# Two graph attention layers on one core: each gather waits for the landing of the third gather ahead of it

## The reference

```python
def layer0(x, src, dst):                 # edges sorted by dst
    h = layer_norm(x); q, k, v = h @ Wq + bq, h @ Wk + bk, h @ Wv + bv
    e = sum(q[dst] * k[src], -1) / 4     # per head, logits of each edge
    p = exp(e - segment_max(e, dst)[dst])
    a = p / segment_sum(p, dst)[dst]
    x = x + segment_sum(a * v[src], dst) @ Wo + bo
    return x + gelu(layer_norm(x) @ W1 + bf1) @ W2 + bf2

def layer1(x, src, dst, edge_attr):
    e = edge_attr @ We                   # added to k[src] and to v[src]
    ...                                  # the same attention, skip, norms and a feed-forward part
x = layer_norm(x + layer0(x, src, dst))
x = layer_norm(x + layer1(x, src, dst, edge_attr_64))
```

## Time and profile before

| what | before |
|---|---|
| median of three runs | 1345.44 us (1345.04 to 1345.83) |
| span of the profiled execution, from the first to the last instruction | 1659.7 us |
| VectorE busy in that span | 1039.2 us, 63% |
| TensorE busy | 914.0 us, 55% |
| GpSimd busy, 832 gathers among it | 898.0 us, 54% |
| ScalarE busy | 749.2 us, 45% |
| steady rounds of layer 0, batches 4 to 25 | 154 to 697 us |
| steady rounds of layer 1, batches 4 to 25 | 945 to 1523 us |

### The profile page before, as it was taken

One profiled execution on the slowest core, in us unless ns is written; L12 is line 12 of the kernel. 1 busy time (PEld: TensorE's weight loads), 2 busy tenths in 40 slices (PEclk: granted clock), 3 DMA queues, 4 the chain that ended last, 5 costly groups with the idle time before them and its releaser, 6 DMA issues. The chain is left out here.

```text
span 1659.7 us, 24287 instructions
## 1 busy us (share of the span) xinstructions
PE 914.0 (55%) x5107; PEld 810.4 (49%) x5107; DVE 1039.2 (63%) x2702; ACT 749.2 (45%) x2535; POOL 898.0 (54%) x1008
## 2 busy tenths in 40 slices
PE   4412545445546545558953455646555565655685
PEld 2312545445545445557833444545455554645574
DVE  4512756656656656686643566766667666667866
ACT  3111455455455454475510245444444444445675
POOL 4656556656656656602347555555655556553054
PEclk9655677767676776678987678777787777777898
DMA  6546766666666666630245566766667666676101
GB/s 190 164 123 136 248 183 205 183 186 207 181 186 207 185 184 204 189 131 14 68 150 156 179 196 177 221 199 203 207 184 217 194 205 184 208 218 196 50 2 39
DMA packets 227719, 280.46 MB, mean 169 GB/s; under 512 B 48261, under 2 KB 176419, under 8 KB 224118
## 3 DMA queue, kind: packets, MB, share of 16 engines
q1 hardware_dynamic: 185808, 167.97, 33.5%
q0 software_dynamic: 39936, 109.11, 21.8%
q10 hardware_dynamic: 1830, 1.86, 0.4%
HBM read 239.72 MB, written 39.08 MB: 168 GB/s over the span
## 5 line engine op out<-in xcount | busy, mean ns | idle before, releaser
L553 POOL DMA_INDIRECT KV<-kv_table,idx x832 | 797.8, 959 | 539.2 <-issue 391.3
L851 PE MATMUL PS<-QW,OHT 128*128 128x128 f32 x1664 | 318.0, 353 | 265.2 <-DVE PR L1143 115.9
L851 PEld LDWEIGHTS PS<-QW,OHT 128*128 128x128 f32 x1664 | 290.2, 261 | 283.5 <-issue 271.3
L896 PE MATMUL PS<-OH,KV 128*128 128x128 f32 x1600 | 268.0, 330 | 104.3 <-ACT AGG L679 49.7
L679 ACT ACTIVATE AGG<-AGG,PC,RCS x800 | 309.8, 387 | 2.0 <-ACT AGG L675 1.0
L896 PEld LDWEIGHTS PS<-OH,KV 128*128 128x128 f32 x1600 | 252.3, 244 | 115.1 <-issue 112.1
L671 ACT ACTIVATE PC<-PS 128x4 f32<-128x4 f32 x200 | 34.2, 171 | 577.0 <-remote 406.0
L1136 DVE TENSOR_TENSOR KV<-KV,PS 128x1024 f32<-128x1024 f32 x104 | 125.9, 1211 | 211.3 <-remote 150.0
L675 ACT ACTIVATE AGG<-PS 128x127 f32 x800 | 209.1, 261 | 1.0 <-issue 0.9
L1143 DVE TENSOR_TENSOR PR<-KV,PS 128x512 f32<-128x512 f32 x208 | 141.2, 679 | 98.3 <-remote 76.7
L871 PE MATMUL PS<-ident,AL 128*128 128x128 f32 x52 | 24.4, 468 | 298.8 <-DVE AL L1230 183.1
(11 more groups left out here) (162 smaller groups left out, 1250.5 us busy)
## 6 DMA issues: line engine op xcount, KB each, us to landing
QW<-q_table SPq DMA_DIRECT2D x832, 64.0 KB
REL<-rel_dram SPq DMA_DIRECT2D x52, 512.0 KB
window_dram<-OH SPq DMA_DIRECT2D x25, 1024.0 KB
OH<-window_dram SPq DMA_DIRECT2D x50, 512.0 KB
KV<-kv_table,idx POOLq DMA_INDIRECT x832
EA<-in_edge_batch SPq DMA_DIRECT2D x52, 256.0 KB
kv_table<-KV SPq DMA_DIRECT2D x24, 256.0 KB, 2.2
q_table<-KV SPq DMA_DIRECT2D x24, 128.0 KB, 2.2
```

The source lines that it names most:

```text
L553: g.indirect_dma_start(KV[:, s, j, :], None, kv_table, bass.IndirectOffsetOnAxis(ap=idx[:, s, j:j + 1], axis=0)).then_inc(gathered[s][hh], 16)
L851: last = te.matmul(o, OHT[:, q // 2, e0:e0 + P], QW[:, n % 2, 4 * q + m, :], start=True, stop=True)
L896: last = te.matmul(PS[4 + q % 2][:, m * P:(m + 1) * P], KV[:, n % SLOTS, j, D:2 * D], at[:, j * P:(j + 1) * P], start=True, stop=True)
```

## The change

The semaphores of the gathers are no longer kept by slot and half. Three are used in turn (IN_FLIGHT = 3): gather number `tile`, counted through both layers, raises semaphore `tile % 3`, and before it is issued GpSimd waits until the gather three before it, the last one on the same semaphore, has landed. Where the landing of a gather is waited for, `landed(tile)` gives the counts of all three semaphores at which every gather up to `tile` has landed; VectorE and SyncE wait for the three. The gathers, their order, the buffers and the other waits stay as they are.

```diff
+IN_FLIGHT = 3
...
-        gathered = [[sem(f"gathered{s}{hh}") for hh in range(2)] for s in range(SLOTS)]
+        gathered = [sem(f"gathered{r}") for r in range(IN_FLIGHT)]
+
+        def landed(tile):
+
+            return [(gathered[r], 16 * ((tile - r) // IN_FLIGHT + 1)) for r in range(IN_FLIGHT)]
...
                 def indices(n):
-                    s, u = n % SLOTS, n // SLOTS + uses[n % SLOTS] * l
+                    s = n % SLOTS
                     if l or n >= SLOTS:
-                        sp.wait_ge(gathered[s][1], u * 128)
+                        last = G * l + n - SLOTS if n >= SLOTS else max(k for k in range(G) if k % SLOTS == s)
+                        for at, count in landed(last * J + J - 1):
+                            sp.wait_ge(at, count)
...
                         for j in range(hh * 8, hh * 8 + 8):
+                            tile = T * l + n * J + j
+                            if tile >= IN_FLIGHT:
+                                pool.wait_ge(gathered[tile % IN_FLIGHT], 16 * (tile // IN_FLIGHT))
                             g.indirect_dma_start(KV[:, s, j, :], None, kv_table,
-                                                 bass.IndirectOffsetOnAxis(ap=idx[:, s, j:j + 1], axis=0)).then_inc(gathered[s][hh], 16)
+                                                 bass.IndirectOffsetOnAxis(ap=idx[:, s, j:j + 1], axis=0)).then_inc(gathered[tile % IN_FLIGHT], 16)
...
                 def add_edges(n, q):
-                    s, u = n % SLOTS, n // SLOTS + 1 + uses[n % SLOTS] * l
+                    s = n % SLOTS
                     if q % 2 == 0:
-                        dve.wait_ge(gathered[s][q // 2], u * 128)
+                        for at, count in landed(T * l + n * J + 4 * q + 7):
+                            dve.wait_ge(at, count)
```

## The result

The kernel after takes 1572.74 us (median; 1563.5 to 1579.88) against 1345.24 us (1344.55 to 1345.83) of the kernel before: a ratio of 1.168, 95% interval 1.165 to 1.171, or 227.5 us more. The forecast was 1415 us, with a range up to 1500.

What follows compares the result with a forecast made beforehand. No engine was taken as full; GpSimd's slack in a plain 19.5 us round decided. Landing waits in bursts, +2 us over 44 rounds, 88 us, less 20 us of lead gave 68: 1345 + 70 = 1415 us, range 1300 to 1500.

Steps and rivals of the forecast that it cites:

- GpSimd's free time: GpSimd's slack in a plain round of gathers, put between nothing and 4.3 us of a 19.5 us round.
- the first rival: GpSimd's gathers already set the pace, so bursts cost full price: some 1500 us; chance 0.20.
- The lead of 20 us: Gathers running ahead of their readers absorb some 10 us of delay a layer, 20 us off the price.
- The price of a burst: Gathers held back during SyncE's big transfers: 3.7 us late once a round, taken as +2 us a round.
- one such place a round: In each round's burst of SyncE transfers, one gather starts 3.7 us late, waiting for the third ahead.
- The parts of the price: For a gather's landing wait: 2.5 us to land plus 0.8 us from count to next start.
- Counts and waits at nothing: VectorE's and SyncE's added conditions and the satisfied waits before GpSimd's gathers were taken to cost 0.
- The 66 us: Upper cost of satisfied waits before 829 gathers, at 0.08 us each, kept only for the range.
- full price: The burst delay with no lead to absorb it: 44 rounds of 3.7 us, 163 us.
- TensorE's counts come sooner: With GpSimd's queue running empty in bursts, TensorE's counts reach waiting engines earlier: 1300 us; chance 0.26.
- The rule on the queues: DMA engines alternate between queues packet by packet, so gathers keep a share in bursts; the prediction's trace disagreed, 0 of 131.

Runs made afterwards that it cites:

- before_again: The kernel before, unchanged, profiled once more: 1348.61 us timed, profile span 1346.5 us.
- fewer: The kernel before with 7 instead of 8 gathers in each half of every batch but the first four: 1266.71 us against 1345.88.
- thin_after: The kernel after with SyncE's big transfers of a round cut to 16 of 128 partitions: 1388.5 us against 1346.97 for the kernel before.
- thin_before: The kernel before with SyncE's big transfers of a round cut to 16 of 128 partitions: 1345.68 us, ratio 0.9994.
- cap8: The kernel after with IN_FLIGHT = 8 instead of 3: 1346.32 us, ratio 1.0014 to the kernel before.
- old_wait: The kernel before plus, ahead of each gather, a wait for the same half two batches earlier, long landed: 1345.12 us against 1345.88.

## Why the prediction was wrong

**The step that failed first: GpSimd's free time.** From the earlier trace rows I took gaps of 2.6 us at each half, put a plain round at 19.5 us between 18.3 and 20.6, and left open whether GpSimd has nothing or up to 4.3 us to spare. It has nothing: 448.0 / 22 = 20.4 and 445.3 / 22 = 20.2 us a round, sixteen turns of 1.25 us and little more (windows of before_again; fewer). So the first rival had the right mechanism, "GpSimd already sets the plain pace", to which I gave 0.20, and its condition, that the 0.30 us between gathers stand in a plain run too, holds. What should have weighed more is the span of 1659.7 us against a median of 1345: a profile 23% longer than the runs isn't one of those runs, and slack read from it isn't theirs. I scaled its rounds down and kept its gaps, and let a turn shrink to 0.95 us although no row had one under 1.25. What could be carried over was the turn itself: 16 x 1.25 us was the sum for which the prediction had a row, and it was right.

**The lead of 20 us** falls with it: VectorE waits for gathers before as well (187.4 us), so no lead is there to eat.

**The price of a burst, mis-sized.** The mechanism was right, a gather held back by the landing of the third ahead while SyncE's transfers run (thin_after and thin_before show it: without them 41.5 us of the 227.5 are left), but "one such place a round" of 3.7 us was too little for layer 1. I read the burst in layer 0 and took layer 1 to be milder; it has the longer one: the slowest gather of a round takes some 8 us there against 5.3 in layer 0 (medians, after), and 5.8 us a round are lost against 2.8. In the burst shown the edge features, the windows and `REL` come together; which of them makes it longer wasn't tried. I also stopped at the first late gather: the ones behind it wait in turn (five in the timeline above, and 215 waits in 52 rounds where I expected one or two a round). And I counted 44 rounds where all 52 pay: the first four batches of each layer gave 34.6 us. So even the full price of the first rival, 163 us, was 64 us short of the 227.5, and the time lay beyond the range.

**The parts of the price.** I put 2.5 us to land and 0.8 us from count to start; it is 2.7 to 2.8 us to the last increment and 0.26 us from there. The sum, 3.0 against 3.3, kept the conclusion: quiet turns stay at 1.25 us, as the timeline of after shows. Taking 0.8 from GpSimd's answer to TensorE's counts was wrong for a wait for a landing, and that answer came from the long execution.

**Counts and waits at nothing: right.** cap8, with more conditions than after, is at most 0.25% above before, and old_wait at most 0.12%. The 66 us that I kept for the waits were not needed.

**The rival "TensorE's counts come sooner"** drew on waits of ScalarE and VectorE for held-back counts. In before_again and in after a matmul's count is recorded within 0.02 us of its end (99 of 100 counts in the steady rounds of layer 0). In the long profile fewer than 2 in 10 are, and more than half come 3 us or more after the end (one count in seven has no record of its own there). So plain runs have nothing of it to give back. The prediction itself named such holds as a possible reason for the 314 us of the long profile, which no run shows; its chance of 0.26 was far too high for a thing that only that profile showed.

**The rule on the queues.** The Trainium skill ("DMA: Bandwidth & Descriptors", section "Queues, rings and completion order") has an engine go round robin between its queues, packet by packet. After's trace doesn't bear out an even share: 63 of 382 packets in a burst were the gathers', 12.3% of the engines' time against 61.0% for SyncE's queue, with two to three gathers pending, and 0 of 131 in the earlier trace rows. How the engines choose wasn't tried.

## What to carry to other kernels

Compare a profile's span with the timed median before reading slack from it; where they differ by a fifth, take the busy time and the turn of the issuing engine, which came out the same here in the long execution and the plain ones, and mistrust the gaps. A cap on transfers in flight was free here where cap times the issue period exceeded the longest landing plus the 0.26 us to restart (8 x 1.25 = 10 us against the 9.6 + 0.26 of after), and the longest landing is that of the worst burst of the worst stage, not the quiet one. Where the issuing engine sets the pace, what landings miss that bound by is added to the time, here to within some 10 us at every cap, and issuing less gained 0.82 us for each gather that isn't there.

## What was not expected of the hardware

A gather blocked on a landing starts 0.258 us after the last increment of that semaphore; in after this is the same to a few ns from the 5th to the 95th percentile of 181 waits with over 0.45 us of idle time. The wait itself, when satisfied, costs too little to be measured (old_wait). A gather of 128 rows of 1 KB lands 2.7 us after its start when the queues are quiet and 8 us after it in a burst of layer 1, although GpSimd needs the same 0.95 us for it. And an unchanged kernel can leave a profile 23% longer than its timed runs, with TensorE's counts held back for microseconds, once in four profiles; the other three, of the same kernel, were plain.
